# A gated attention layer: 36 of a group's 48 context products alternate one by one with the products of three W tiles

## The chip, the cores and the metric

The kernel runs on one core of one Trainium2 chip. Its engines are PE (TensorE, matmuls; its weight loads are shown as PEld), DVE (VectorE), ACT (ScalarE), POOL (GpSimd) and SP (SyncE, which here issues DMAs). They run side by side and order their work by semaphores: an instruction waits until a counter has reached a value, and another raises the counter when it is done. Each engine takes its own instructions in program order. The metric is the device time of one execution in microseconds (us), the median of several.

## What is computed

x and the context are 64 x 128 x 512 in float32. Cut to what matters here:

```python
def xattn(x, k, v, Wh, wg_w, wo_w, gamma, beta):     # k = v = context
    Q, K, V = (einsum('bshd,hde->bshe', t, Wh) for t in (xh, kh, vh))    # 4 heads of 128
    scores = einsum('bshe,bthe->bhst', Q, K) / sqrt(hd)
    A = maximum(abs((scores * D).sum(axis=0)), 1.0)   # summed over all 64 batches
    O = einsum('hst,bthe->bshe', A, V)
    Y = (O - mean) / sqrt(var + 1e-3) * gamma + beta
    return relu(x @ wg_w) * Y @ wo_w

x = x + tanh(g_xattn) * xattn(layernorm(x), ctx, ctx, ...)
x = x + tanh(g_ffn) * ffn(layernorm(x), gate, up, down, ...)    # 512 -> 1408 -> 512
```

The attention matrix A needs the sum over all 64 batches, so the kernel has a first part that goes through every batch, and only then can make O. The change is in the first part only.

## The kernel before

The 64 batches (tiles, t) are taken in 16 groups g of four. For each group the first part makes, from the normalized and transposed x (xnt) and the transposed context (ct):

- **z**, four sets of products, z(4g) to z(4g+3), one for each head: x times Wh Wh^T. Three float16 products of 512 columns each (high by high, high by low, low by high), written to the two PSUM banks pz[0] and pz[1] in turn (both lie in the tensor po). ACT copies the high part out (z_hi, L710), DVE makes the low part (z_lo, L1129), which also frees the bank: z(n) waits for z_lo(n-2).
- **v**, one per tile: for each of four heads three products in float32 (two parts of ct by 256 columns, of which 128 are Wh and 128 are z), into ps[t % 2]. v(t, 0) is heads 0 and 1, v(t, 1) heads 2 and 3: six products each, 48 a group. v(t, half) waits for the z_lo of its heads, for ct_lo (POOL), and for the bank: v_out(t-2) and v_acc(t-2). ACT's v_out (L735) copies V out of the bank to tmp, v_store (L747) sends it to the scratch in DRAM, and DVE's v_acc (L1159) adds the scores to a sum.
- **w**, one per tile: relu(x @ wg). Four blocks k of three float16 products of 512 columns into the bank pyb; ACT's w_out (L743) takes the relu to tmp, and w_store (L751) sends it off. w(t) waits for w_out(t-1).
- **rows(u)**, one per two tiles: four small transposes that spread mean and 1/std (POOL's rstd_pair) into ptb. DVE's normal(u) (L1125, four operations) then normalizes the transposed x, ACT's x_hi (L700) and POOL's x_lo (L1715) split it into xnt for the next group, and z of the next group waits for the last x_lo.
- ct_hi (ACT, L706) and ct_lo (POOL, L1721) split the context of the next group.

The order of every engine is written out by hand. On PE, group g (1 to 13) is: z(4g), z(4g+1), rows(2g+2), three blocks of w(4g-1), z(4g+2), z(4g+3), the last block of w(4g-1), v(4g, 0), v(4g+1, 0), v(4g, 1), v(4g+1, 1), rows(2g+3), w(4g), v(4g+2), w(4g+1), v(4g+3), w(4g+2). In group 1 rows(5) comes behind w(4). Group 14 has only two w tiles there, group 15 is shorter. LATE is 58; the w tiles from there on come behind the groups.

DVE's order in a group is: z_lo(4g), z_lo(4g+1), normal(2g+2), z_lo(4g+2), z_lo(4g+3), low_sums (some groups), stats(4g+8), v_acc(4g), v_acc(4g+1), normal(2g+3), stats, scale_tops (g = 10) or scale_powers (g = 13), low_weights(g-2, 0) (g = 2 to 13: L1213, and for the first eight chunks also L1222), wo_limit, wg_top (g = 8, 9), v_acc(4g+2), stats, low_sums (some), v_acc(4g+3), stats(4g+11) (g up to 13), low_weights(g-2, 1), wo_lo (L1245, g = 4 to 7) or wg_top (L1248, g = 8, 9). These side jobs look at the weights of the second part. stats are L1101 and L1103.

ACT's order is: four z_hi, w_out(4g-1), x_hi, w_store, x_hi, v_out(4g), v_out(4g+1), the two v_store, two ct_hi, w_out(4g), x_hi, w_store, x_hi, v_out(4g+2), w_out(4g+1), v_store, v_out(4g+3), w_store, v_store, wo_hi (g = 3 to 6), two ct_hi, w_out(4g+2), w_store.

SP loads the context and x for the coming groups, each load as soon as its buffer is free (for the context: when ct_lo is done), and for g = 9 to 13 parts of down_t that low_weights looks at.

## Time and profile before

| | us |
|---|---|
| three runs | 1441.26, 1441.88, 1445.92 |
| median | 1441.88 |
| span of the profiled execution | 1447.4 |
| PE busy in it | 1420.4 (98%) |
| PE weight loads (PEld) | 728.3 (50%) |
| DVE | 1043.3 (72%) |
| POOL | 735.3 (51%) |
| ACT | 726.3 (50%) |
| first part, groups 1 to 14 (34.07 to 311.66) | 277.6 |

The page's busy line for PE is at nine tenths or more in nearly every fortieth of the span, and the granted clock is near full throughout. Of the chain that ended last 74% is PE's. A busy share is a mean over stages, so the rows below are of the stage that the change touches. Matmuls overlap: one lasts 0.38 us in a row, but the next starts after 0.216 us, so starts are to be compared, not durations. A group of matmuls in the timeline runs until the start of the next, not for the duration shown. After a wait, or behind a product of another kind, the recorded start of a v product can be early.

### The profile page before, as it was taken

How to read it: one execution, taken by the hardware profiler on the slowest of the kernel's cores; microseconds unless marked ns; L12 is line 12 of the kernel's file. 1: busy time of each engine (PE TensorE's matmuls, PEld its weight loads, DVE VectorE, ACT ScalarE, POOL GpSimd, SP SyncE). 2: the span in 40 equal slices, each digit the busy share in tenths (PEclk: the TensorE clock that was granted, in tenths of full speed). 3: DMA queues.
4: the chain of work that ended last, by engine and by line, in shares of the span. 5: the costliest groups of instructions: out<-in, count | busy, mean ns of one | idle time of the engine just before them, and what ended most of it. 6: DMA issues, size and time to landing. Idle time of an engine off the chain costs nothing.

```text
span 1447.4 us, 20320 instructions
## 1 busy us (share of the span) xinstructions
PE 1420.4 (98%) x7097; PEld 728.3 (50%) x7135; DVE 1043.3 (72%) x1562; ACT 726.3 (50%) x1145; POOL 735.3 (51%) x734
## 2 busy tenths in 40 slices
PE   8999999999999999999999999999999999999998
PEld 4666666665445544455444444444444444444443
DVE  7788998878477676766776677564867768768762
ACT  5566565554555635455463545534344444443442
POOL 5656769863564445444553554434137237137235
PEclk9999999999999999999999999999999999999999
DMA  8999898973878796987888897886383473572432
GB/s 275 344 336 306 292 317 318 343 251 130 276 204 263 227 276 206 260 276 210 248 274 237 264 243 222 247 252 164 112 228 115 124 224 122 139 218 98 139 109 89
DMA packets 372920, 324.96 MB, mean 225 GB/s; under 512 B 259280, under 2 KB 285264, under 8 KB 372816
## 3 DMA queue, kind: packets, MB, share of 16 engines
q1 hardware_dynamic: 355248, 291.63, 66.2%
q10 hardware_dynamic: 17568, 31.99, 6.2%
q8 instruction: 59, 0.97, 0.3%
q14 instruction: 45, 0.37, 0.1%
HBM read 209.14 MB, written 114.43 MB: 224 GB/s over the span
## 4 chain that ended last, share of the span: by engine, by line
PE 74%; DVE 10%; DMA 6%; SPq 3%; issue 3%; ACT 2%; POOL 2%; ACTq 0%; DVEq 0%; POOLq 0%
PE ps L2067 24%; PE po L2067 8%; PE pyb L1930 7%; PE ps L2074 7%; PE ptb L2074 5%; PE pyb L2074 5%; PE ps L1988 5%; PE po L1930 3%; PE pyb L2058 3%; PE ptb L2058 3%; DMA wy_scratch<-misc 2%; SPq L510 2%; DVE reg L1129 1%; PE ptb L2062 1%; PE pyb L2062 1%
## 5 line engine op out<-in xcount | busy, mean ns | idle before, releaser
L2067 PE MATMUL ps<-x2t,gate 128*128 128x512 f16 x704 | 166.6, 379 | 1.2 <-DVE tmp L1436 1.1
L1930 PE MATMUL pyb<-xnt,wgs 128*128 128x512 f16 x708 | 166.3, 380 | 1.4 <-DVE wgs L1153 1.3
L2067 PE MATMUL ps<-op,wbuf 128*128 128x512 f16 x704 | 166.3, 379 | 0.5 <-issue 0.5
L2067 PE MATMUL ps<-x2t,up 128*128 128x512 f16 x704 | 166.3, 379 | 0.0
L1800 POOL TENSOR_TENSOR p5b<-p5b,p1b 128x512 f32<-128x512 f32 x44 | 55.7, 1265 | 209.1 <-ACT p5b L860 209.1
L1816 POOL TENSOR_TENSOR hid<-tmp,hid 128x512 f16<-128x512 f32 x88 | 104.6, 1190 | 105.9 <-ACT hid L836 105.9
L2074 PE MATMUL ps<-down_first,hid 128*128 128x512 bf16 x683 | 152.4, 379 | 2.1 <-POOL hid L1816 0.8
L1811 POOL TENSOR_TENSOR hsp<-hall,hsp 128x640 f16<-128x640 f32 (+2 forms) x72 | 123.6, 1731 | 37.1 <-ACT hsp L887 37.1
L2067 PE MATMUL po<-op,wbuf 128*128 128x512 f16 x528 | 129.0, 379 | 0.6 <-DVE u2b L1383 0.6
L1436 DVE SCALAR_TENSOR_TENSOR tmp<-ps,colsb,tmp 128x512 f32<-128x512 f32 x88 | 65.4, 744 | 68.2 <-PE ps L2067 62.3
L1988 PE MATMUL ps<-reg 128*128 128x256 f32 x768 | 109.7, 294 | 4.3 <-DVE reg L1129 3.8
L2067 PEld LDWEIGHTS ps<-op,wbuf 128*128 128x128 bf16 x704 | 68.5, 98 | 84.4 <-issue 2.5
L1760 POOL TENSOR_TENSOR wy_part<-raw,wy_part 128x1024 f16<-128x1024 f32 x30 | 66.0, 2201 | 87.6 <-ACT wy_part L825 87.6
L2067 PEld LDWEIGHTS ps<-x2t,up 128*128 128x128 bf16 x704 | 68.8, 98 | 82.9
L907 ACT ACTIVATE tmp<-ps,colsb 128x512 f32<-128x512 f32 x88 | 60.3, 685 | 99.2 <-PE ps L2067 99.1
L2074 PEld LDWEIGHTS ps<-down_first,hid 128*128 128x128 f16 x704 | 68.1, 98 | 83.4 <-POOL hid L1816 2.0
L2067 PEld LDWEIGHTS ps<-x2t,gate 128*128 128x128 bf16 x704 | 67.0, 98 | 81.0 <-DVE tmp L1436 1.8
L1988 PEld LDWEIGHTS ps<-reg 128*128 128x128 f32 x768 | 98.4, 190 | 13.3 <-DVE reg L1129 5.7
L1930 PEld LDWEIGHTS pyb<-xnt,wgs 128*128 128x128 f16 x708 | 66.4, 98 | 73.7 <-DVE wgs L1153 2.6
L1721 POOL TENSOR_TENSOR reg<-raw,reg 128x512 fp32r<-128x512 f32 x60 | 75.4, 1280 | 39.5 <-ACT reg L706 39.5
L1403 DVE TENSOR_TENSOR nbuf<-po,p1b 128x512 f32<-128x512 f32 x44 | 30.4, 692 | 78.5 <-PE po L2067 78.5
L887 ACT CAST hsp<-hall 128x640 f16<-128x640 f32 (+2 forms) x72 | 48.7, 712 | 71.2 <-PE pyb L2074 36.7
(218 smaller groups left out, 2764.2 us busy)
## 6 DMA issues: line engine op xcount, KB each, us to landing
wbuf<-ws_scratch SPq DMA_DIRECT2D x44, 896.0 KB, 5.0
xr<-in_x SPq DMA_DIRECT2D x62, 512.0 KB, 6.3
raw<-in_ctx_t SPq DMA_DIRECT2D x32, 512.0 KB, 5.6
v_scratch<-tmp ACTq DMA_DIRECT2D x64, 256.0 KB, 6.0
raw<-v_scratch SPq DMA_DIRECT2D x32, 512.0 KB, 6.6
x_scratch<-xr SPq DMA_DIRECT2D x32, 512.0 KB, 4.8
xr<-x_scratch SPq DMA_DIRECT2D x32, 512.0 KB, 5.9
raw<-w_scratch SPq DMA_DIRECT2D x31, 512.0 KB, 6.0
```

The source lines that it names most:

```text
L907: e.activation(tmp[:, m % 3, :], banks[2 * (n % 2)], ACT.Silu, scale=colsb[:, j:j + 1]).then_inc(s["si"])
L1436: e.scalar_tensor_tensor(tmp[:, m % 3, :], banks[2 * (n % 2) + 1], colsb[:, NI + j:NI + j + 1], tmp[:, m % 3, :], ALU.mult, ALU.mult).then ...
L1721: e.tensor_tensor(ct[g % 2][1][:, h, :], raw[:, h, :], f(ct[g % 2][0][:, h, :]), ALU.subtract).then_inc(s["ctlo"])
L1760: e.tensor_tensor(wyt[1][:, :, :], wt_of(q), wyt[0][:, :, :], ALU.subtract).then_inc(s["wylo"])
L1800: e.tensor_tensor(p5b[n % 2][:, :], p5b[n % 2][:, :], p1b[n % 2][:, :], ALU.add).then_inc(s["p15"])
L1811: e.tensor_tensor(hsp[t % 2][1][:, i0:i1, :], hall[:, i0:i1, 128 * i:128 * i + 128], hsp[t % 2][0][:, i0:i1, :], ALU.subtract).then_inc(s[ ...
L1816: e.tensor_tensor(hid[1][m % 11], tmp[:, m % 3, :], hid[0][m % 11], ALU.subtract).then_inc(s["hlo"])
L1930: last = e.matmul(dst, lhs[a], rhs[b], start=(k == 0 and i == 0), stop=(k == n - 1 and i == 2))
L1988: last = e.matmul(ps[t % 2][:, h, :, :], ct[g % 2][i][:, h, 128 * b:128 * b + 128], wh_and_z(q, h, b), start=(n == 0), stop=(n == 2))
L2058: e.matmul(py(t), wyt_of(t)[0][:, k, :], wos[i][k], start=(k == 0 and i == 0), stop=False)
L2067: last = e.matmul(dst, upper(wt), act[i], start=start, stop=stop and exact, skip_group_check=True)
L2074: last = e.matmul(dst, act, packed, start=start, stop=stop and exact)
```

## The change

It touches PE's order, ACT's order and the banks of W. In the full groups (g = 1 to 13) v(4g+1, 0), v(4g, 1), v(4g+1, 1), v(4g+2, 0), v(4g+2, 1) and v(4g+3, 0), 36 products, alternate one by one with the 36 products of w(4g), w(4g+1) and w(4g+2). v(4g, 0) stands alone ahead of them and v(4g+3, 1) behind them. rows(2g+3) comes in the middle. Group 14 has 18 such pairs. w(4g) and w(4g+1) (tiles 4 to 56) go to the banks pz[0] and pz[1] of z, so w(4g) waits for z_lo(4g+2), w(4g+1) for z_lo(4g+3), and z(4g+4), z(4g+5) wait for w_out(4g), w_out(4g+1). w(4g+2) and w(4g+3) stay in pyb. On ACT, w_out(4g) goes between v_out(4g) and v_out(4g+1), w_out(4g+1) ahead of v_out(4g+2), and two ct_hi, wo_hi and w_out(4g+2) ahead of v_out(4g+3). The order of DVE, POOL and SP is the same. The computation is the same.

```diff
         def pw(t):
+            if 4 <= t < LATE - 1 and t % 4 < 2:
+                return pz[t % 4]
             if t <= LATE:
                 return pyb[:, :]
@@ ACT, group g
-                v_out(4 * g)
-                v_out(4 * g + 1)
+                if more and g < NG - 2:
+                    v_out(4 * g)
+                    w_out(4 * g)
+                    v_out(4 * g + 1)
+                else:
+                    v_out(4 * g)
+                    v_out(4 * g + 1)
...
                 if g < NG - 2:
-                    w_out(4 * g)
+                    w_store(4 * g)
                 x_hi(2 * g + 3, 0)
-                if g < NG - 2:
-                    w_store(4 * g)
                 x_hi(2 * g + 3, 1)
+                w_out(4 * g + (1 if g < NG - 2 else 0))
                 v_out(4 * g + 2)
-                w_out(4 * g + (1 if g < NG - 2 else 0))
+                w_store(4 * g + (1 if g < NG - 2 else 0))
                 v_store(4 * g + 2)
-                v_out(4 * g + 3)
-                w_store(4 * g + (1 if g < NG - 2 else 0))
-                v_store(4 * g + 3)
+                ct_hi(g + 1, 2)
+                ct_hi(g + 1, 3)
                 if 3 <= g < 7:
                     wo_hi(g - 3)
-                ct_hi(g + 1, 2)
-                ct_hi(g + 1, 3)
                 if g < NG - 2:
                     w_out(4 * g + 2)
+                v_out(4 * g + 3)
+                if g < NG - 2:
                     w_store(4 * g + 2)
+                v_store(4 * g + 3)
@@ PE, z(n)
+                if h < 2 and 8 <= n < LATE + 3:
+                    p.wait_ge("wev", n - 3)
@@ PE, v(t, half, beside)
+                if beside:
+                    w_ready(*beside)
+                for n in range(6):
+                    h, (i, q) = 2 * half + n // 3, ((0, 0), (1, 0), (0, 1))[n % 3]
+                    last = e.matmul(ps[t % 2][:, h, :, :], ct[g % 2][i][:, h, 128 * b:128 * b + 128],
+                                    wh_and_z(q, h, b), start=(n % 3 == 0), stop=(n % 3 == 2))
+                    if half and n == 5:
+                        last.then_inc(s["v"])
+                    if beside:
+                        w_term(beside[0], beside[1][n // 3], n % 3)
+
+            def w_ready(t, ks):
                 x_ready(t // 4)
-                if 0 < t <= LATE:
+                if t in (1, 2, 3):
+                    p.wait_ge("wev", t)
+                elif 4 <= t < LATE - 1:
+                    p.wait_ge(*(("zlo", t + 3) if t % 4 < 2 else ("wev", t - 2) if t % 4 == 2 else ("wev", t)))
+                elif LATE - 1 <= t <= LATE:
                     p.wait_ge("wev", t)
@@ PE, group g
-                if g > 1:
-                    rows(2 * g + 3)
-                if g < NG - 2:
-                    w(4 * g)
-                if g == 1:
-                    rows(5)
-                v(4 * g + 2, 0)
-                v(4 * g + 2, 1)
-                w(4 * g + (1 if g < NG - 2 else 0))
-                v(4 * g + 3, 0)
+                full = g < NG - 2
+                v(4 * g, 0)
+                v(4 * g + 1, 0, (4 * g, (0, 1)) if full else None)
+                v(4 * g, 1, (4 * g, (2, 3)) if full else None)
+                v(4 * g + 1, 1, (4 * g + 1, (0, 1)) if full else (4 * g, (0, 1)))
+                rows(5 if g == 1 else 2 * g + 3)
+                v(4 * g + 2, 0, (4 * g + 1, (2, 3)) if full else (4 * g, (2, 3)))
+                v(4 * g + 2, 1, (4 * g + 2, (0, 1)) if full else None)
+                v(4 * g + 3, 0, (4 * g + 2, (2, 3)) if full else (LATE - 1, (0, 1)))
                 v(4 * g + 3, 1)
-                if g < NG - 2:
-                    w(4 * g + 2)
-                else:
-                    w(LATE - 1, (0, 1))
```

## Rows read from the trace of the kernel before

**Rows 1.** By group: us, busy (x) PE, PEld, DVE, ACT, POOL; PEclk, DMA share, GB/s.

```profile
134.31:154.81 20.50, 19.86 (x117) 12.61 (x116) 18.08 (x32) 12.79 (x24) 15.48 (x15) 1.00 0.88 296
...
294.07:311.66 17.59, 16.35 (x100) 10.81 (x99) 15.41 (x26) 9.93 (x17) 14.91 (x13) 1.00 0.61 202
sum 277.59, PE 273.06 PEld 175.70 DVE 240.97 ACT 166.57 POOL 203.37; mean PE 19.50 PEld 12.55 DVE 17.21 ACT 11.90 POOL 14.53
```

**Rows 2.** Timeline of DVE and of PE in a heavy group; start us, us, what, idle before.

```profile
135.50 1.84 DVE L1245 SCALAR_TENSOR_TENSOR wos<-up,wo_lim,wos 128x512 f16<-128x512 f32 x1
137.27 1.27 DVE L1129 TENSOR_TENSOR reg<-po,reg 128x512 fp32r<-128x512 f32 x2
...
142.18 1.70 PE L1988 MATMUL ps<-reg 128*128 128x256 f32 x12 [0.64 <-DVE reg L1129]
```

**Rows 3.** Timeline of PE around the start of group 10.

```profile
212.24 2.76 PE L1930 MATMUL pyb<-xnt,wgs 128*128 128x512 f16 x12
214.84 1.46 PE L1930 MATMUL po<-xnt,gs 128*128 128x512 f16 x6
...
218.51 1.46 PE L1930 MATMUL po<-xnt,gs 128*128 128x512 f16 x6
219.81 0.81 PE L1930 MATMUL pyb<-xnt,wgs 128*128 128x512 f16 x3
220.27 3.22 PE L1988 MATMUL ps<-reg 128*128 128x256 f32 x24
223.33 0.38 PE L1950 MATMUL ptb<-ident,mv 128*128 128x128 f32 x2
```

**Rows 4.** Timeline of DVE over the same stretch.

```profile
213.05 0.69 DVE L1159 TENSOR_TENSOR misc<-misc,ps 128x512 f32<-128x512 f32 x1 [0.24 <-ACT tmp L735]
...
214.48 0.85 DVE L1213 TENSOR_REDUCE lowbits<-up 128x1 f32<-128x704 uint16 x1
...
216.74 1.29 DVE L1129 TENSOR_TENSOR reg<-po,reg 128x512 fp32r<-128x512 f32 x2
217.95 2.47 DVE L1125 TENSOR_TENSOR xn<-xn,ptb 128x512 f32<-128x512 f32 x4
220.34 1.28 DVE L1129 TENSOR_TENSOR reg<-po,reg 128x512 fp32r<-128x512 f32 x2
```

**Rows 5.** Timeline of PE and of its weight loads (PEld), short windows at two edges.

```profile
206.56 0.38 PE L1930 MATMUL pyb<-xnt,wgs 128*128 128x512 f16 x1
...
206.89 0.19 PEld L1988 LDWEIGHTS ps<-reg 128*128 128x128 f32 x1
...
208.08 0.28 PE L1988 MATMUL ps<-reg 128*128 128x256 f32 x1
...
208.20 0.10 PEld L1930 LDWEIGHTS pyb<-xnt,wgs 128*128 128x128 f16 x1
...
208.43 0.10 PEld L1930 LDWEIGHTS pyb<-xnt,wgs 128*128 128x128 f16 x1
```

**Rows 6.** Timeline of ACT, the copy v_out(39).

```profile
212.43 0.58 ACT L735 COPY tmp<-ps 128x512 f32<-128x512 f32 x1 [0.74 <-PE ps L1988]
```

**Rows 7.** Stores of V from tmp, 102.9 to 292.3 us: issue to landing.

```profile
DMA to landing us min/median/max: 2.0/6.2/10.2
```

**Rows 8.** Timeline of DVE in groups 10 and 13, the two blocks of scales.

```profile
228.79 0.80 DVE L1168 SCALAR_TENSOR_TENSOR mags<-colsb 128x22 f32<-128x22 f32 x1
...
231.46 0.88 DVE L1213 TENSOR_REDUCE lowbits<-misc 128x1 f32<-128x704 uint16 x1
...
287.69 1.50 DVE L1188 TENSOR_REDUCE inv<-tops 128x6 f32<-128x768 f32 x1
...
292.19 0.87 DVE L1213 TENSOR_REDUCE lowbits<-misc 128x1 f32<-128x704 uint16 x1
```

**Rows 9.** A long gap of PE, and granted clock (PEclk) in the stage behind it.

```profile
772.14 2.15 PE L2058 MATMUL pyb<-wos,wy_part 128*128 128x512 f16 x6 [2.77 <-ACT wy_part L825]
...
772.00:776.00 4.00, 3.86 (x11) 1.52 (x12) 3.93 (x6) 1.03 (x2) 3.75 (x3) 0.60 0.85 142
```

More of the change, by code:

```diff
@@ L1923, in _, with three @@
             p = Program(e, s)
-            def three(dst, lhs, rhs, k, n, low=None):
+            def three(dst, lhs, rhs, k, n):
                 for i, (a, b) in enumerate(((0, 0), (0, 1), (1, 0))):
-                    if i == 2 and low:
-                        p.wait_ge(*low)
                     last = e.matmul(dst, lhs[a], rhs[b], start=(k == 0 and i == 0), stop=(k == n - 1 and i == 2))
@@ L1974, in first_z, with v @@
                             last.then_inc(s["z"])
-            def v(t, half):
+            def v(t, half, beside=None):
                 g, b = divmod(t, 4)
@@ L1985, in v @@
                     p.wait_ge("acc", t - 1)
-                for h in (2 * half, 2 * half + 1):
-                    for n, (i, q) in enumerate(((0, 0), (1, 0), (0, 1))):
-                        last = e.matmul(ps[t % 2][:, h, :, :], ct[g % 2][i][:, h, 128 * b:128 * b + 128],
-                                        wh_and_z(q, h, b), start=(n == 0), stop=(n == 2))
-                if half:
-                    last.then_inc(s["v"])
-            def w(t, ks=range(4)):
-                x_ready(t // 4)
-                if 0 < t <= LATE:
+                if beside:
[9 more added lines that the diff above has]
+            def w_ready(t, ks):
+                x_ready(t // 4)
+                if t in (1, 2, 3):
[3 more added lines that the diff above has]
+                elif LATE - 1 <= t <= LATE:
                     p.wait_ge("wev", t)
@@ L2003, in w, with w_term @@
                     p.wait_ge("vev", B)
-                for k in ks:
-                    if t == 0:
-                        p.wait_ge("scaledhi", k + 2)
-                    last = three(pw(t), [q[:, k, 128 * (t % 4):128 * (t % 4) + 128] for q in wgs],
-                                 [q[:, k, :] for q in xnt[t // 4 % 2]], k, 4, ("scaledlo", k + 2) if t == 0 else None)
-                if 3 in ks:
-                    last.then_inc(s["w"])
+            def w_term(t, k, i):
+                a, b = ((0, 0), (0, 1), (1, 0))[i]
+                if t == 0:
+                    p.wait_ge("scaledhi", k + 2)
+                    if a:
+                        p.wait_ge("scaledlo", k + 2)
+                last = e.matmul(pw(t), wgs[a][:, k, 128 * (t % 4):128 * (t % 4) + 128], xnt[t // 4 % 2][b][:, k, :],
+                                start=(k == 0 and i == 0), stop=(k == 3 and i == 2))
+                if k == 3 and i == 2:
+                    last.then_inc(s["w"])
+            def w(t, ks=range(4)):
+                w_ready(t, ks)
+                for k in ks:
+                    for i in range(3):
+                        w_term(t, k, i)
             def o(q):
@@ L2280, in _ @@
                     w(4 * g - 1, (3,))
-                v(4 * g, 0)
-                v(4 * g + 1, 0)
-                v(4 * g, 1)
-                v(4 * g + 1, 1)
                 if not more:
+                    v(4 * g, 0)
+                    v(4 * g + 1, 0)
+                    v(4 * g, 1)
+                    v(4 * g + 1, 1)
                     w(LATE - 1, (3,))
@@ L2291, in _ @@
                     break
-                if g > 1:
-                    rows(2 * g + 3)
-                if g < NG - 2:
-                    w(4 * g)
-                if g == 1:
-                    rows(5)
-                v(4 * g + 2, 0)
-                v(4 * g + 2, 1)
-                w(4 * g + (1 if g < NG - 2 else 0))
-                v(4 * g + 3, 0)
+                full = g < NG - 2
+                v(4 * g, 0)
+                v(4 * g + 1, 0, (4 * g, (0, 1)) if full else None)
[5 more added lines that the diff above has]
+                v(4 * g + 3, 0, (4 * g + 2, (2, 3)) if full else (LATE - 1, (0, 1)))
                 v(4 * g + 3, 1)
-                if g < NG - 2:
-                    w(4 * g + 2)
-                else:
-                    w(LATE - 1, (0, 1))
             w(LATE)
```

## The prediction

> **What bounds the kernel now.** I read the stages first, then the order of work inside one group, then the waits at its edges. The view of the groups takes the stretches from one z(4g) to the next; group k stands for g = k. Groups 1 to 14 take 277.59 us, and PE is busy in 273.06 of it, while DVE is busy 240.97 [rows 1]. A light group takes 19.58 us with no gap on PE; a heavy one (134.31 to 154.81) takes 20.50 [rows 1], and the 0.92 more is one gap, in which v(4g, 1) waits for z_lo(4g+3) (ahead of 142.18) [rows 2]. So the first part is PE's, with DVE just behind it in groups 5 to 8. The rest of the kernel isn't touched, and I move it whole.
>
> Inside a group: z(4g), z(4g+1), rows(2g+2), nine products of w(4g-1), then z(4g+2) comes 3.67 us after z(4g) (214.84 to 218.51); z, z and three w products more take 1.95; then 24 v products from 220.46 (219.81 plus three w at 0.216) to 223.33, which is 0.1195 us each; a w product takes 0.216 (six z in 1.30) [rows 3]. The last twelve w products of the group start at 212.24, so the last v is done 2.6 us before the next group starts at 214.84 [rows 3]. DVE's order is fixed by its program: v_acc(4g+3), stats, low_weights(g-2, 1), wo_lo or wg_top, and only then z_lo of the next group. In the trace v_acc(39) starts at 213.05, that is 1.79 before the group, low_weights at 214.48, z_lo(40) at 216.74, normal at 217.95, z_lo(42) at 220.34 [rows 4].
>
> **The change, part by part. 1, the pair on PE.** Each full group (g = 1 to 13) turns 36 v products in runs into v, w, v, w. No row shows such a row of singles, but both of its edges are there. A weight load starts with the product ahead of its own, so a load's start marks that product's start. From a w to a v: the last w starts at 206.56, the second v at 206.89, and 0.334 is 0.216 + 0.118: the f32 weights of the first v are loaded behind the w. From a v to a w: the v starts at 208.08, the f16 load only at 208.20, and the second w at 208.43, so v and w together take 0.349 instead of 0.120 + 0.216 [rows 5]. I found the same 0.348 to 0.349 at every one of these edges, also where the load has no wait of its own. Weights in f16 are thus not loaded while an f32 v product streams, and a v ahead of a w costs 0.133, 0.013 more than a v ahead of a v. 36 pairs cost 36 x 0.013 = 0.47 more per group, 6.3 us in 13 full groups and the 18 pairs of group 14. The bounds: if the load hides, the v takes the 0.109 of 256 columns (half of 0.216 and a little), the pair 0.325 and the group 36 x 0.024 = 0.86 less than I say; above, nothing points past 0.349. I take 0.349, since its rows are the very pair.
> The Trainium skill (TensorE: Matmul & The Clock Gate, "What happens when you issue a matmul") says the next tile's weights load while the current matmul runs, through a read port of their own. By it the pair would be 0.325. The rows at 208.08 to 208.43 don't agree for f32 followed by f16.
>
> **2, where the last v goes.** This is the large term, and it isn't on PE. Before, w(4g+2) came after v(4g+3, 1). Now it is woven in before it, and v(4g+3) ends where the next group begins. v_out starts 0.32 after the last v product starts (that is 0.13 ahead of the w at 212.24, so 212.11, and v_out 212.43 [rows 6]), and v_acc 0.62 after v_out (213.05). The last v product starts 0.13 before the new group, so v_acc(4g+3) can start 0.81 after the group's start, where it stood 1.79 before it: 2.6 us later. Nothing in DVE's program was moved, so all that is queued behind v_acc comes later by as much. Let A be the start of z_lo(4g), counted from z(4g). A = 0.81 + 1.43 for v_acc and stats (213.05 to 214.48) = 2.24; plus low_weights 1.56 (of 214.48 to 216.74, the rest is wg_top) where it has both reductions (groups 3 to 10) or 0.80 with one (11 to 14); plus wo_lo 1.77 (137.27 less 135.50, groups 5 to 8) or wg_top 0.70 (9 and 10) [rows 2, 4].
> z(4g+2) needs z_lo(4g) and can start 0.74 after it starts. In groups 5 to 8 that was met to the tick (137.27 + 0.74 = 138.01, the group's start plus 3.69). Now PE waits there: A + 0.74 against 3.68.
>
> **3, the new wait of w(4g).** It writes the bank of z(4g+2), so v(4g+1, 0) with its first w waits for z_lo(4g+2), which DVE starts 3.60 after z_lo(4g) because normal(2g+2) lies between (216.74 to 220.34 [rows 4]). PE may go on at A + 3.60 + 0.74 = A + 4.34. Queued behind that wait are all later products of the group. PE itself would be there at A + 0.74 + 1.95 + 0.72 = A + 3.41, so this costs 0.93 more in a group already late. What follows is 18 pairs (6.27), rows (0.44), 18 pairs, six v (0.73): 13.7. The period of a full group is therefore A + 18.05. The old wait of v(4g, 1) for z_lo(4g+3), worth 0.9 in groups 5 to 7, 0.5 in 8 and 0.9 in 11, is covered: v(4g, 1) now comes 2.1 us later.
>
> **4, ACT, POOL, SP.** Let V be the start of v(4g, 0). Six v and 18 pairs later, less the last pair, v(4g+1) is done; v_out takes it at V + 7.0, v_acc at 7.6, normal(2g+3) starts at V + 8.2 (rows(2g+3) is done by 7.7) and ends at 10.6; x_hi ends about V + 11.2, x_lo about V + 13.5 (two at 1.15), and z needs it at V + 14.5. This is nothing, by 1 us. ACT then has v_out(4g+2) at 11.8, two ct_hi, w_out(4g+2) at 13.9, v_out(4g+3) at 14.65: on time, except that wo_hi (0.6, groups 4 to 7) now stands ahead of the last two and delays them 0.45. v_store(4g) has 4.1 us until v_out(4g+2) wants its buffer; such stores landed in 2.0 to 10.2, median 6.2 [rows 7], and the long ones fall beside SP's loads, which now come only at V + 10.7 or later, behind ct_lo(g+1, 1). I take nothing, and up to 1.2 us a group for the upper bound.
>
> **5, DVE late in the middle.** normal(2g+3) ends at V + 10.6; stats, low_weights, wg_top, v_acc, stats and low_sums follow. In g = 8 and 9 they end 0.57 after v_acc(4g+3) could start. In g = 10 the scales (228.79 to 231.46, 2.67) make it 1.75, and the load of down_t that low_weights waits for another 0.75. In g = 13 scale_powers (287.69 to 292.19, 4.50) makes it 3.7 [rows 8].
>
> **The sum.** Periods A + 18.05: group 2 (A 2.24) 20.3; 3 (3.8) 21.9; 4 (4.25) 22.3; 5 to 7 (6.0) 24.1 each; 8 (5.6) 23.6; 9 and 10 (5.05) 23.1 each; 11 (5.5) 23.6; 12 and 13 (3.5, with 0.45 for the load) 21.5 each. Group 1 21.3 (only the new wait, about half a us). Group 14 keeps 12 v products together, A is 7.1 and the rest 13.8: 20.9 against 17.59 [rows 1]. Together 315.4, less 277.59, is 37.8; group 15 gives back 0.5, since it waited for late z_hi. Of the 37.8 some 6 are the pairs on PE, the others waits.
> The clock: PE will stand 2.6 to 3.6 us at z(4g+2) in groups 5 to 8 and 14. Once the trace shows such a gap, 2.77 us before 772.14, and behind it the granted clock is 0.60 in 772 to 776, the lower level 1.2 GHz for most of it [rows 9]: about 1.7 us lost. Here at most five such gaps, and the wait for z_lo(4g+2) takes up 0.9 of each loss; I add 1 us of a possible 8. The Trainium skill (TensorE: Matmul & The Clock Gate, "Why this matters for your kernels") warns of gaps of this length, and the row agrees.
> The execution profiled has a span of 1447.4 and the runs a median of 1441.88, 5.5 less; the differences are of one execution's groups and carry over. 1441.9 + 38 = 1480.
>
> **Rivals.** (a) The pair is 0.325 and the waits are as above: 36 x 0.024 x 13, and 0.4 in group 14, give 11.6 back: 1468. For it: the w-to-v edge hides its load. Against: every v-to-w edge [rows 5]. (b) PE alone counts: the waits on DVE don't appear, because v_acc isn't as late as I put it. Then 6 us for the pairs, less some 5 for the old waits: within 1442 to 1450. Against: six v products are all that PE does after the last woven pair. (c) Dearer: stores land late for v_out and w_out (1.2 us in ten groups) or the clock falls at all five gaps: 1492 to 1500. (d) The other side: the f16 load hides behind v. Before, the v's were bound by their loads (0.120 against 0.109), so 486 pairs save 0.011 each, 5.3 us, and the old z_lo(4g+3) waits of 5 go too: 1431. It decides only if z_lo(4g) starts within 2.94 us of the group, and with low_weights A is 3.8 in all of groups 3 to 10. (e) The change does what it says; PE's order can't be otherwise.
>
> **How the numbers follow.** Forecast 0.62, (a) 0.15, (b) 0.07, (c) 0.12, (d) 0.04. The range goes from 1460, (a) with a few us less of waits, to 1494, the lower part of (c); outside lie (b), (d) and half of (c). About 0.3% (4 us) is what a measurement here can tell from no change. Faster 0.04 is (d); same 0.03 is part of (b); slower 0.93.
>
> **What would show it.** On PE single v and w in turn, 0.349 from v to v (0.325 by (a)). A gap ahead of z(4g+2), released by z_lo, of 2.3 to 3.1 us in groups 5 to 8 and near 0 in group 2; a second of 0.9 at v(4g+1, 0). v_acc(4g+3) 0.8 after z of the next group. Periods of 21 to 24 us. The prediction is wrong if the periods stay near 20: then DVE had the z_lo's done earlier than its program order lets me think, or v_out didn't come last.

## The result, and the profile after

The changed kernel takes 1483.21 us (median; 1480.43 to 1484.19) against 1442.49 for the kernel before on the same chip (1441.26 to 1445.92): a ratio of 1.0277, 95% interval 1.0259 to 1.0296. It is slower by 40.7 us; 1480 was forecast, in a range of 1460 to 1494.

The head of the page of the kernel after: busy time of each engine, share of the span, instructions; then the chain that ended last by engine; then the line of v.

```profile
PE 1429.8 (96%) x7097; PEld 722.5 (49%) x7135; DVE 1038.7 (70%) x1562; ACT 725.4 (49%) x1145; POOL 734.5 (50%) x734
...
PE 69%; DVE 13%; DMA 5%; ACT 4%; issue 3%; SPq 3%; POOL 2%; ACTq 0%; DVEq 0%
...
L1997 PE MATMUL ps<-reg 128*128 128x256 f32 x768 | 213.1, 403 | 12.1 <-DVE reg L1135 10.2
```

The stages of the kernel after, with columns as in [rows 1]: a heavy group (6), a light one (12), group 14, all of groups 1 to 14, and the rest.

```profile
144.86:167.95 23.09, 20.47 (x119) 12.22 (x117) 16.99 (x32) 12.59 (x24) 15.22 (x15) 1.00 0.71 259
...
284.35:305.56 21.21, 20.36 (x119) 12.22 (x118) 15.13 (x27) 11.56 (x21) 17.33 (x16) 1.00 0.83 301
326.77:349.58 22.81, 17.65 (x101) 11.10 (x100) 18.15 (x29) 10.62 (x19) 17.47 (x14) 0.93 0.52 173
34.94:349.58 314.64, 283.61 (x1607) 170.06 (x1608) 236.01 (x423) 165.86 (x294) 202.38 (x192) 0.99 0.77 278
349.58:1482.30 1132.72, 1116.49 (x5337) 535.74 (x5372) 775.58 (x1085) 540.01 (x814) 513.81 (x514) 1.00 0.69 202
```

Groups 1 to 14 took 277.59 us before [rows 1] and take 314.64: 37.05 more, of which PE is busy for 10.6 (283.61 less 273.06) and idle for the other 26.5. DVE has the same instructions in them and is busy for 5 us less (236.01 against 240.97; 3.8 of the 5 are the four wo_lo, which last shorter, see part 2 below), so the loss isn't work, it is order. Another 0.9 lies ahead of group 1, where the executions of all kernels here differ by as much. The rest of the kernel is 3.0 shorter than in the profiled execution of before, which was 5.5 us above its own median. In the fourteen profiled executions of this study the rest takes 1129.0 to 1135.7 us, and that of the kernel before is the longest, so I read nothing into the 3.0.

Which waits they are, by the view of waits of the whole kernel after (line, waited for, us in total, times, longest):

```profile
PE po L1934 <- DVE reg L1135: 19.6, 13, 3.5
PE ps L1997 <- DVE reg L1135: 10.2, 12, 0.9
...
PE ps L1997 <- ACT tmp L745: 1.6, 1, 1.6
```

The first two, z and v waiting for z_lo, are 1.4 and 3.8 us in the kernel before. They stand at the two places that the prediction names: ahead of z(4g+2) in groups 1, 3 to 11 and 14, and at v(4g+1, 0) in all full groups but 2 (0.85 each). The third is a single wait for w_out(56) in group 14, which nobody forecast. The timeline of PE in group 6 (start, us, what, count, idle before):

```profile
146.59 2.11 PE L2027 MATMUL pyb<-xnt,wgs 128*128 128x512 f16 x9
150.47 1.47 PE L1934 MATMUL po<-xnt,gs 128*128 128x512 f16 x6 [1.77 <-DVE reg L1135]
...
154.15 0.36 PE L1997 MATMUL ps<-reg 128*128 128x256 f32 x1 [0.85 <-DVE reg L1135]
154.34 0.39 PE L2027 MATMUL po<-xnt,wgs 128*128 128x512 f16 x1
154.38 0.47 PE L1997 MATMUL ps<-reg 128*128 128x256 f32 x1
154.69 0.39 PE L2027 MATMUL po<-xnt,wgs 128*128 128x512 f16 x1
154.73 0.47 PE L1997 MATMUL ps<-reg 128*128 128x256 f32 x1
```

and of DVE in the same group, which began at 144.86:

```profile
146.08 0.69 DVE L1165 TENSOR_TENSOR misc<-misc,ps 128x512 f32<-128x512 f32 x1 [0.94 <-ACT tmp L737]
...
147.50 0.85 DVE L1219 TENSOR_REDUCE lowbits<-up 128x1 f32<-128x704 uint16 x1
148.27 0.88 DVE L1228 TENSOR_REDUCE wmax<-up 128x1 f32<-128x704 f32 x1
149.07 0.74 DVE L1251 SCALAR_TENSOR_TENSOR wos<-up,wo_lim,wos 128x512 f16<-128x512 f32 x1
149.72 1.28 DVE L1135 TENSOR_TENSOR reg<-po,reg 128x512 fp32r<-128x512 f32 x2
...
153.31 1.28 DVE L1135 TENSOR_TENSOR reg<-po,reg 128x512 fp32r<-128x512 f32 x2
```

v_acc(23) starts 1.22 behind the group's start (in the kernel before 1.79 ahead of it [rows 4]), z_lo(24) at 149.72, 4.86 behind it. z(26) starts at 150.47, 0.75 later, and v(25, 0) at 154.15, 0.84 after z_lo(26). The matmul ends are modelled, so I also take what a wait costs from the starts: nine w products from 146.59 would be over at 148.53, so the first costs 1.94; v(25, 0) comes 1.08 later than six v products of 0.120 behind the one before allow.

### The profile page after: what moved, and what is told of

Read it like the earlier page. It is cut to its first block, busy times and chain, and to the rows that moved or that the text cites. A ratio compares the mean times of both kernels' runs of the same rounds, so it can differ in the third digit from the quotient of the medians.

```text
span 1482.3 us, 20333 instructions
## 1 busy us (share of the span) xinstructions
PE 1429.8 (96%) x7097; PEld 722.5 (49%) x7135; DVE 1038.7 (70%) x1562; ACT 725.4 (49%) x1145; POOL 734.5 (50%) x734
## 4 chain that ended last, share of the span: by engine, by line
PE 69%; DVE 13%; DMA 5%; ACT 4%; issue 3%; SPq 3%; POOL 2%; ACTq 0%; DVEq 0%
PE ps L2093 24%; PE po L2093 8%; PE ps L2100 6%; PE ptb L2100 5%; PE pyb L2100 5%; PE po L2027 4%; PE ps L1997 4%; PE pyb L2084 3%; PE ptb L2084 3%; PE po L1934 2%; DMA wy_scratch<-misc 2%; DVE xr L1131 2%; SPq L512 2%; DVE reg L1135 2%; PE pyb L2027 1%
## 5 line engine op out<-in xcount | busy, mean ns | idle before, releaser
L1997 PE MATMUL ps<-reg 128*128 128x256 f32 x768 | 213.1, 403 | 12.1 <-DVE reg L1135 10.2
L1997 PEld LDWEIGHTS ps<-reg 128*128 128x128 f32 x768 | 135.4, 196 | 18.2 <-issue 14.7
L2027 PE MATMUL po<-xnt,wgs 128*128 128x512 f16 x324 | 114.2, 390 | 0.0
L2027 PE MATMUL pyb<-xnt,wgs 128*128 128x512 f16 x384 | 111.6, 384 | 1.2 <-DVE wgs L1159 1.1
L1165 DVE TENSOR_TENSOR misc<-misc,ps 128x512 f32<-128x512 f32 x63 | 43.2, 686 | 76.7 <-ACT tmp L737 76.5
```

Source lines behind the costliest of these rows:

```text
L1997: last = e.matmul(ps[t % 2][:, h, :, :], ct[g % 2][i][:, h, 128 * b:128 * b + 128], wh_and_z(q, h, b), start=(n % 3 == 0), stop=(n % 3 == 2))
L2027: last = e.matmul(pw(t), wgs[a][:, k, 128 * (t % 4):128 * (t % 4) + 128], xnt[t // 4 % 2][b][:, k, :], start=(k == 0 and i == 0), stop=(k ...
```

## The experiments

All ratios are against the kernel before on the same chip (1442 to 1443 us). The runs are spread over several chips, so two experiments are compared by their ratios, or by their traces. "z(60)" is the start of group 15 in the profiled execution: 311.66 in the kernel before, 349.58 in the one after. It measures the part that was changed alone. A is the start of z_lo(4g) counted from the group's start, as in the prediction. Two questions are asked: is it the pairs on PE or the waits on DVE, and is one cause of a wait worth its whole length?

**e1_blocks: 36 edges made 6.** In v(), the w products of a half first, then the v products.

```diff
+                for n in range(6) if beside else ():
+                    w_term(beside[0], beside[1][n // 3], n % 3)
                 for n in range(6):
...
-                    if beside:
-                        w_term(beside[0], beside[1][n // 3], n % 3)
```

> The changed kernel, but each of the six mixed stretches of a group has its six W products first and then its six v products, instead of one by one. All waits, banks and the order of the stretches stay. Edges from a v to a W product fall from 36 to 6 in a group. Theory (the waits on DVE's queue make most of the loss, the pair 0.349 instead of 0.336 the rest): 30 x 0.013 = 0.39 us less in each of 13 full groups, 0.2 in group 14, about 1478 us; the gap ahead of z(4g+2) stays (1.95 us in groups 6 and 7). Rival (alternating one by one is itself what costs, on PE or in the banks): most of the 41 us come back, 1445 to 1455.

Measured: 1482.34 us, ratio 1.0272 (1.0250 to 1.0293), z(60) at 350.24. The 5 us of the theory didn't come, and the rival that saw the pairs as the cause is far off. Group 6, by stage:

```profile
142.54:165.52 22.98, 19.93 (x119) 12.82 (x118) 17.00 (x32) 12.59 (x24) 15.19 (x15) 1.00 0.74 261
```

PE is busy for 0.54 less than in the kernel after (20.47), and the group is only 0.11 shorter (22.98 against 23.09): A has gone from 4.87 to 5.30. From v(4g, 0) to v_acc(4g+3) it is 16.6 us here and 16.7 there (group 6). That stretch, v, v_out, v_acc, normal, x_hi and v again, sets when z_lo can come, and the six v products at the end of each block end as late as those of the pairs do (reckoned: 18 x 0.349 less the last w's 0.216 is 6.07; 18 x 0.336 plus three edges of 0.013 is 6.09). The granted clock also fell behind three gaps (groups 7, 11 and 14), where it fell behind one in the kernel after (group 14), and groups 7 and 11 are 0.5 and 1.4 us longer. The other ten of groups 2 to 13 are together 1.3 shorter, where the theory has 3.9.

**e2_dve: DVE's queue mended.** v_acc(4g-1) behind z_lo(4g), z_lo(4g+1); its stats, low_weights, wo_lo and wg_top behind z_lo(4g+3).

```diff
                 z_lo(4 * g + 1)
+                if g > 1:
+                    v_acc(4 * g - 1)
...
                 z_lo(4 * g + 3)
+                if g > 1:
+                    if n + 3 < B:
+                        stats(n + 3)
+                    if 3 <= g < 15:
+                        low_weights(g - 3, 1)
+                    if 5 <= g < 9:
+                        wo_lo(g - 5)
+                    if g in (9, 10):
+                        wg_top(2 * g - 17)
...
-                v_acc(4 * g + 3)
-                if n + 7 < B:
-                    stats(n + 7)
-                if 2 <= g < 14:
-                    low_weights(g - 2, 1)
-                if 4 <= g < 8:
-                    wo_lo(g - 4)
-                if g in (8, 9):
-                    wg_top(2 * g - 15)
```

> The changed kernel with one difference, on DVE: v_acc(4g-1) stands behind z_lo(4g), z_lo(4g+1) of the next group instead of ahead of them, and stats, low_weights, wo_lo and wg_top of the group before stand behind z_lo(4g+3). PE, ACT and the banks as in the changed kernel. Theory (DVE's queue ahead of z_lo is what PE waits for): z_lo(4g) starts about 1.8 us after the group's start, no gap ahead of z(4g+2) except in groups 11 and 14, a gap of 0.6 at v(4g+1, 0) because v_acc now lies ahead of normal; periods near 20.7, in all some 25 us less, 1458 us (1454 to 1462). Rival (the late z_lo are a symptom, PE or ACT is late by itself): 1478 or more.

Measured: 1469.57, ratio 1.0176 (1.0159 to 1.0193), z(60) at 335.66. The gap at z(4g+2) is gone in groups 2 to 8, A is 1.8 to 2.3 there, and 13.6 us came back: the queue is a cause. But it isn't the 25 us that the sum of the gaps promised, and the reason is in the stages. Group 6, then group 9:

```profile
139.33:160.44 21.11, 20.28 (x119) 12.33 (x117) 18.09 (x32) 12.57 (x24) 15.29 (x15) 1.00 0.80 285
...
202.27:225.94 23.67, 20.63 (x119) 12.16 (x118) 19.78 (x34) 13.36 (x24) 14.29 (x15) 1.00 0.71 252
```

DVE is busy for 18 to 20 us in these groups, and what is moved back in its queue holds up something else. In group 6 v_acc(23) now stands ahead of normal, z_lo(26) starts at 145.81, and v(25, 0) waits 0.83 for it: all of the idle time in that group. Group 9 is a wait of another kind; the timeline of ACT:

```profile
201.77 0.59 ACT L737 COPY tmp<-ps 128x512 f32<-128x512 f32 x1 [2.17 <-DMA v_scratch<-tmp]
...
204.91 0.69 ACT L745 ACTIVATE tmp<-pyb,lim 128x512 f32<-128x512 f32 x1 [1.02 <-DMA w_scratch<-tmp]
```

v_out and w_out wait there for stores to land and free their buffer: the mechanism of rival (c), 3.2 us on ACT; groups 11 to 13 have one such wait each, of 0.8 to 1.5. Once the DVE wait is gone, this is what is next. It kept group 9 dear in the two kernels below that have the same order too (25.03 and 22.95).

**e3_banks: the gate of w(4g).** w(4g) back in pyb, w(4g+1) and w(4g+2) in the two banks of z.

```diff
-            if 4 <= t < LATE - 1 and t % 4 < 2:
-                return pz[t % 4]
+            if 4 <= t < LATE - 1 and t % 4 in (1, 2):
+                return pz[t % 4 - 1]
...
-                if h < 2 and 8 <= n < LATE + 3:
-                    p.wait_ge("wev", n - 3)
+                if h < 2 and 8 <= n < LATE:
+                    p.wait_ge("wev", n - 2)
...
-                    p.wait_ge(*(("zlo", t + 3) if t % 4 < 2 else ("wev", t - 2) if t % 4 == 2 else ("wev", t)))
+                    p.wait_ge(*(("zlo", t + 2) if t % 4 in (1, 2) else ("wev", t - 2) if t % 4 == 3 else ("wev", t)))
```

> The changed kernel with other banks: w(4g) in pyb, w(4g+1) in pz[0], w(4g+2) in pz[1], w(4g+3) in pyb, so w(4g) waits for w_out(4g-1) and no longer for z_lo(4g+2). Theory (that wait costs 1.08 us in every full group, as the trace of the changed kernel shows at v(4g+1, 0)): it goes, and w_out(4g-1), done about 1 us after v(4g, 0) starts, leaves 0.3; 0.75 less in 12 to 13 groups, about 1473 us. Rival (the wait only takes up time that the next one, v(4g, 1) for z_lo(4g+3) or v_acc, would take anyway): 1481 to 1484.

Measured: 1474.47, ratio 1.0211 (1.0180 to 1.0242), z(60) at 343.63: as the theory said. Groups 6 to 10, 12 and 13 are 0.69 to 0.71 shorter with A unchanged (group 6: 22.39, A 4.87). In groups 1 to 5, where A moved by up to 0.7, the gain is 0.96, -0.19, 0.44, 0.84 and 0.57; in group 11 the clock fell. It isn't the whole 1.08, since w(4g) now waits for w_out(4g-1) to empty pyb, 0.40 later than PE could start (row under e11_small_banks).

**e4_lastv: the last v back in its place.** w(4g+2) in one piece behind v(4g+3, 1), and v_out(4g+3) ahead of wo_hi, ct_hi and w_out on ACT. PE's part of the edit:

```diff
-                v(4 * g + 2, 1, (4 * g + 2, (0, 1)) if full else None)
-                v(4 * g + 3, 0, (4 * g + 2, (2, 3)) if full else (LATE - 1, (0, 1)))
+                v(4 * g + 2, 1)
+                v(4 * g + 3, 0)
                 v(4 * g + 3, 1)
+                if full:
+                    w(4 * g + 2)
+                else:
+                    w(LATE - 1, (0, 1))
```

> The changed kernel with only w(4g) and w(4g+1) woven in: v(4g+2, 1), v(4g+3, 0), v(4g+3, 1) stand alone and w(4g+2) behind them, as in the kernel before (group 14 likewise), and v_out(4g+3) stands ahead of ct_hi and w_out(4g+2) on ACT again. So v(4g+3) is done 2.6 us before the next group. Rival, the simple reading of my prediction (the place of the last v is all): z_lo(4g) comes 2.6 us earlier everywhere, 1450 us. Theory with both ends of DVE's queue: rows(2g+3) is still late, normal(2g+3), stats, low_weights, v_acc(4g+2), stats keep DVE busy until about 14.4 us after V, which is the group's end, so v_acc(4g+3) starts only 0.1 after the next group's start, 0.7 to 1.1 us earlier than in the changed kernel in groups 3 to 8, not in 9 to 11; with 12 edges fewer about 1474 us.

Measured: 1476.74, ratio 1.0228 (1.0207 to 1.0250), z(60) at 343.76. The theory's 1474 holds; the simple reading, that the last v's place is the whole loss, is wrong by 27 us. v_acc(4g+3) comes -0.4 to +0.4 from the group's start in groups 2 to 7 (0.55 to 1.22 before this edit), not the -1.79 of the kernel before, and in 8 to 10 no sooner at all: the gate of w(4g) has delayed every v of the group already, and what DVE owes from the middle of the group is still ahead of v_acc. The timeline of ACT and of DVE at the end of group 6 (group 7 starts at 163.53) shows it:

```profile
162.09 0.59 ACT L737 COPY tmp<-ps 128x512 f32<-128x512 f32 x1 [0.46 <-ACT tmp L737]
...
162.46 0.69 DVE L1164 TENSOR_TENSOR misc<-misc,ps 128x512 f32<-128x512 f32 x1
163.07 0.69 DVE L1106 BATCH_NORM_STATS2 st<-xr 128x6 f32<-128x512 f32 x1
...
163.89 0.67 DVE L1164 TENSOR_TENSOR misc<-misc,ps 128x512 f32<-128x512 f32 x1
```

v_out(27) is done at 162.68, but v_acc(27) starts at 163.89, behind v_acc(26) and its stats, with no idle time of DVE before it.

**e5_dve_banks and e7_dve_banks_blocks: mended together.** e5 is the edits of e2 and e3; e7 that and e1's.

> The changed kernel with both the DVE order of e2 and the banks of e3, the alternation one by one kept. Theory (the losses are waits in a loop through DVE): the gap ahead of z(4g+2) and the one at v(4g+1, 0) for z_lo(4g+2) are both gone or small, periods near 20.4 where DVE's middle isn't late (23 in group 9, 21 to 22 in 11, 13 and 14): about 1457 us. Rival (e2 and e3 take the same time away twice): 1468 or more.

Measured: 1467.51, ratio 1.0179 (1.0162 to 1.0195), z(60) at 335.57. Not 1457; the rival, one and the same slack, fits better, and the ratio can't be told from that of e2 (1.0176). Groups 2 to 8 are up to 0.6 shorter than in e2, 2.2 us in all, and group 9 (25.03 for 23.67) takes 1.4 of it back: z(37) waits 2.72 us there for w_out(34), which comes behind two waits of ACT for stores, and the granted clock is 0.57 in the 4 us behind that gap.

> As e5_dve_banks, with each mixed stretch as six W products and then six v products (as in e1). In e1 the 30 edges fewer gave no time back, since PE was waiting anyway. Theory (the pair's price of 0.013 us counts only where PE is the bound): here most periods are PE's, so 0.39 in some 8 to 10 groups, 3 to 4 us less than e5. Rival (the price isn't real, or is paid elsewhere): no difference, or more.

Measured: 1466.40, ratio 1.0167 (1.0152 to 1.0183), z(60) at 331.67, 3.9 sooner than in e5. In the trace the edges come through where PE is nearer to being the bound (group 3: 19.90 against 20.46), but 2.1 of the 3.9 lie in group 9, where the clock didn't fall this time. The medians of the two kernels are 1.1 apart with intervals that overlap, so I call this seen in one trace each, not measured.

**e6_before_dve: e2's order of the late jobs in the kernel before.** stats, low_weights, wo_lo and wg_top of the end of a group behind z_lo(4g+3) of the next, v_acc where it was (the lower half of e2's diff, without its v_acc lines).

> The kernel before with one change, on DVE: stats(4g-1), low_weights(g-3, 1), wo_lo and wg_top of the group before stand behind z_lo(4g+3) instead of ahead of z_lo(4g). PE, ACT, banks as before. Theory (even before, v(4g, 1) waits 0.9 us in groups 5 to 7, 0.5 in 8 and 0.9 in 11 for z_lo(4g+3), because these jobs stand ahead of it): these gaps go, periods 19.6, 4 to 5 us less than before, 1438 us. Rival (DVE is full in groups 5 to 9 in any order, 18.1 to 19.7 us busy in periods of 19.6 to 20.5): the gaps move to another place, within 1.5 us of before.

Measured: 1456.78, ratio 1.0102 (1.0084 to 1.0121): 14 us slower, and both sides missed it. The stage of group 8, and what PE waited for in it:

```profile
177.62:198.94 21.32, 20.04 (x118) 12.65 (x117) 19.30 (x32) 11.76 (x20) 14.77 (x15) 1.00 0.93 343
...
190.79 1.67 PE L1989 MATMUL ps<-reg 128*128 128x256 f32 x12 [1.17 <-DVE misc L1159]
```

The wait for z_lo(4g+3) went, as expected, and v(4g+2) now waits 1.17 for v_acc(4g). In its new place wo_lo runs beside POOL and lasts 1.68 (186.70), where alone it lasts 0.74 (see e8 and e9 below); that is 0.94 of the 1.17. So even in the kernel before DVE's queue has no place where 2 us of work can be put for nothing. A price read off as "work moved to where DVE is idle" was wrong twice, here and in e2.

**e8_small and e9_before_small: the side jobs cut, after and before.** In low_weights and low_sums, `704 * half + 704`, `stg[:, :]` and `n * quarter + n` become 64 columns; most of the look at W's low bits and maxima is left out. DVE's queue keeps its order and loses some 1.3 us of work ahead of z_lo(4g) where both reductions stand there.

> The changed kernel with DVE's side jobs low_weights and low_sums cut to 64 columns each (from 704, 640 or 768), so they leave out most of the look at the weights' low bits and maxima; nothing else differs. Theory (DVE's queue): low_weights falls from 1.56 to about 0.3, z_lo(4g) comes 1.3 us earlier in groups 3 to 10, the gap ahead of z(4g+2) goes in groups 3, 4 and 12, 13 and shrinks to 0.4 in 5 to 8; the 1.08 at v(4g+1, 0) stays in part: about 1460 us. Rival (PE order and banks by themselves): above 1478.

Measured: 1466.13, ratio 1.0176 (1.0145 to 1.0208), z(60) at 335.12: 17 us back, 6 fewer than the theory's 1460, and far from the rival. In groups 6 and 7 A falls only from 4.87 to 4.64, because wo_lo moves beside POOL (next rows).

> The kernel before with the look at W's low bits and maxima cut to 64 columns of each piece, as e8_small did to the kernel after: most of that look is left out. It says what the side jobs of VectorE cost the order before. Theory: in the kernel before they cost only the waits of 0.9 us in groups 5 to 8 and 11, so 1438 us, and the 23 us by which e8_small stands above the kernel before are the price of the new order itself. Rival: they cost the old order nothing either, 1442 to 1443. If it came to 1425 or less, the side jobs would bind the old order as well and the comparison with e8_small would have to be read anew.

Measured: 1439.58, ratio 0.9979 (0.9966 to 0.9991), z(60) at 308.46, as the theory said (1438). All full groups from 2 on now take 19.58 to 19.65. The same jobs cost the new order 17 us and the old one 3. That is the finding of the study in one pair: the jobs lay hidden behind PE, and the change uncovered them. It isn't the whole loss: the ratio of e8_small is still 1.0176.

This pair also shows what made wo_lo cost 1.8 us at one time and 0.7 at another. Timeline of DVE and POOL in e8_small:

```profile
143.05 1.84 DVE L1251 SCALAR_TENSOR_TENSOR wos<-up,wo_lim,wos 128x512 f16<-128x512 f32 x1
...
141.84 2.50 POOL L1727 TENSOR_TENSOR reg<-raw,reg 128x512 fp32r<-128x512 f32 x2
```

and in e9_before_small:

```profile
134.90 0.74 DVE L1245 SCALAR_TENSOR_TENSOR wos<-up,wo_lim,wos 128x512 f16<-128x512 f32 x1
...
135.04 2.96 POOL L1721 TENSOR_TENSOR reg<-raw,reg 128x512 fp32r<-128x512 f32 x2 [1.56 <-ACT reg L706]
```

Started while the first of ct_lo's two pieces runs on POOL, wo_lo lasts 1.84 and ends 0.55 behind the second; started 0.14 ahead of ct_lo it lasts 0.74, and the two pieces last 2.96 where they last 2.50 in e8_small. The Trainium skill (SBUF — State Buffer, "Who interferes with whom") says that a VectorE instruction with two inputs in SBUF and a GpSimd one that reads SBUF can't run side by side: whichever is issued second waits for the first. The rows of e9 agree: the first piece of ct_lo, begun behind wo_lo, lasts 1.74 for the second's 1.26. In e8 wo_lo waits for the piece that was running, as the page says, but also through the second piece, whose record starts 0.02 behind its own; that sentence doesn't explain the second wait.

**e10_before_zlo: a candidate.** The kernel before, in groups 5 to 8, 11 and 14 both z_lo's ahead of normal(2g+2).

```diff
-                if more:
+                first = g in (5, 6, 7, 8, 11, 14)
+                if more and not first:
                     normal(2 * g + 2)
                 z_lo(4 * g + 2)
                 z_lo(4 * g + 3)
+                if more and first:
+                    normal(2 * g + 2)
```

> The kernel before, in whose groups 5 to 8, 11 and 14 VectorE makes z_lo(4g+2) and z_lo(4g+3) ahead of the normalization of rows 2g+2, not behind it. Theory: v(4g,1) no longer waits 0.9 us there for z_lo, six groups at 0.9, and the normalization comes late enough to be needed by nobody sooner: 1438 us. Rival: VectorE has no slack there; what it does later for the rows makes the transposes or v_lo wait, and the time stays within 1.5 us of the kernel before or is slower, as with e6_before_dve.

Measured: 1444.37, ratio 1.0024 (1.0011 to 1.0038): the rival, by 2.1 us. The wait at v(4g, 1) went and another came, in group 6:

```profile
143.48 0.40 PE L1953 MATMUL ptb<-ident,mv 128*128 128x128 f32 x2 [0.37 <-DVE xr L1125]
```

the transposes for rows 2g+3, which want the normalization of rows 2g+2 done. DVE also stood idle 0.94 for z_hi ahead of z_lo(4g+2). Groups 1 to 14 take 277.5 us, as before (277.6). No kernel here beats the one before with all its work in place.

**e11_small_banks and e12_small_banks_blocks: what is left when DVE is out of the way.** e8's cut with e3's banks, and e12 with e1's blocks as well.

> The kernel after with the banks of e3_banks and the side jobs of VectorE cut as in e8_small (most of the look at W's low bits and maxima is left out). What is left against e9_before_small is the interleaving itself and the order of VectorE. Theory: the wait of w(4g) for z_lo is gone (0.7 us a group as in e3_banks): e8_small's 1466 less 7 to 8 is 1459 us. Rival: without the side jobs the gate was not the last thing to come, within 2 us of e8_small.

Measured: 1462.30, ratio 1.0136 (1.0115 to 1.0157), z(60) at 328.97, 6.2 sooner than e8_small; by the medians 3.8 less, half of the 7 to 8 expected, with intervals that overlap (1.0115 to 1.0157 against 1.0145 to 1.0208).

> As e11_small_banks, but each mixed stretch runs its six W products first and then its six context products, so 6 edges from context to W a group and not 36. Theory: with the side jobs and the bank wait gone TensorE is nearer to being the bound, and 30 edges at 0.013 us are 0.39 us in each of some 8 groups: 3 us less than e11_small_banks, 1456 us. Rival: the round of v_out, v_acc, normalization and v_out still sets the period, and the two kernels differ by less than 1 us, as e1_blocks and the kernel after did.

Measured: 1460.71, ratio 1.0131 (1.0114 to 1.0148), z(60) at 327.33. Over the whole kernel 1.6 us against 3, less than these intervals can tell. Light groups are clear, though. Group 12 of e9, of e11 and of e12:

```profile
252.53:272.11 19.58, 19.58 (x117) 12.72 (x116) 13.46 (x27) 11.66 (x20) 17.17 (x16) 1.00 0.96 325
...
265.99:286.44 20.45, 20.29 (x119) 12.33 (x118) 13.37 (x27) 11.53 (x21) 17.39 (x16) 1.00 0.84 310
...
263.34:283.24 19.90, 19.74 (x119) 12.86 (x118) 13.33 (x27) 11.34 (x21) 17.31 (x16) 1.00 0.86 322
```

Here PE has one short wait and no other, in e11 at

```profile
272.64 0.35 PE L1997 MATMUL ps<-reg 128*128 128x256 f32 x1 [0.16 <-ACT tmp L745]
```

which by the starts costs 0.40 (0.32 in e12). 19.58 + 0.40 + 36 x 0.013 is 20.45, what the group takes; with 6 edges 19.58 + 0.32 + 0.08 is 19.98 against 19.90. So an edge costs about what the prediction said, where PE is the bound. Beside that, e11 stands 20.5 us behind e9 at z(60): 12 groups at 0.87 are 10.4, group 14 is 5.4 (22.07 against 16.70), and the rest (less 0.9 in group 1) lies mostly in groups 5 to 7 and 11, where A still reaches 3.6 to 4.65.

## Why the prediction held, point by point

**The place of the loss** held. It was to be waits on z_lo and not PE's own time, and of the 37.05 us in groups 1 to 14 PE's busy time is 10.6.

**Part 1, the pair** held in size: from 154.38 to 154.73, 0.35, and sixteen pairs from 154.38 to 159.96 are 0.349 each. The weight loads in the same stretch tell why:

```profile
154.34 0.10 PEld L2027 LDWEIGHTS po<-xnt,wgs 128*128 128x128 f16 x1
154.34 0.20 PEld L1997 LDWEIGHTS ps<-reg 128*128 128x128 f32 x1
154.69 0.10 PEld L2027 LDWEIGHTS po<-xnt,wgs 128*128 128x128 f16 x1
```

The f32 load starts with the w product ahead of it (154.34), the f16 load only when that w product is due itself (154.69), not with the v product at 154.38. What failed is how the term was used. The 6.3 us were added to the waits as if they were apart from them. e1_blocks took 30 of the 36 edges away and gained 0.9 us (within the error), e11 against e12 shows the full price only in light groups. Rival (a), a pair of 0.325, is ruled out by the measured 0.349, and what it would have given isn't shown: with it the v products of each stretch would also have ended sooner (18 x 0.325 less 0.216 is 5.63, for 6.07), which e1's blocks don't do.

**Part 2, the queue** held, but for one term and one sign. For group 6, forecast and measured:

```
                                          forecast  measured
v_acc(4g+3) behind the group's start        0.81      0.81 (light groups)
wo_hi ahead of v_out(4g+3) on ACT           0.45      0.41 (1.22 in groups 4, 6, 7)
v_acc and stats                             1.43      1.42
low_weights, two reductions                 1.56      1.57
wo_lo                                       1.77      0.65   <- mis-sized
A                                           6.02      4.87
A to the next group's start (P - A)        18.05     18.22
period P                                   24.1      23.09
```

The mis-sized term is wo_lo. The row at 135.50 with its 1.84 us was taken for its duration. It was a duration with POOL in the way: ct_lo ran from 134.29 for 2.50 us in the kernel before, and in the kernel after, 3.0 us later against the group's start, wo_lo starts when ct_lo (146.52, two of 1.28) is through, and takes 0.74 in all four groups. This makes four groups 0.9 to 1.2 too dear in the forecast, 4.1 us together, and with it the sign that was to show it, a gap of 2.3 to 3.1 us ahead of z(4g+2) in groups 5 to 8, failed: the gaps are 1.35 to 1.78. One row of a two-input DVE instruction should have been compared with POOL's rows over the same stretch. The part also gave one reason for the late v_acc, the place of the last v. e4_lastv shows a second that reaches nearly as far: with the last v back, DVE's own jobs from the middle of the group still hold v_acc(4g+3) until -0.4 to +0.4 of the next group's start, where it stood at -1.79.

**Part 3, the gate** held: 1.08 in each full group from 3 on, for 0.93. e3_banks took 0.68 of it away (0.40 was left) and got 0.69 to 0.71 in seven groups: with A unchanged this wait is on the path by itself, unlike the pairs.

**Part 4** held in these groups: a store made v_out wait once in the kernel after (0.27 us at 324.50, in group 13), and x_hi and x_lo came in time. Waits of rival (c)'s kind, 1.2 us a group, were seen once e2 let PE run faster: 2.17 and 1.02 in one group, 0.8 to 1.5 in three more.

**Part 5**, DVE late in the middle, was too cheap in group 11: 24.48 for 23.6, with A at 6.27 for 5.5 (v_acc starts 2.68 behind the group's start). Group 14 took 22.81 for 20.9, but not by its A, which is 6.62 where the forecast puts 7.1 (its own terms, 2.24 + 0.80 + 3.7, give 6.74). What follows z_lo took 16.2 for 13.8. Timeline of PE, and in the last line the granted clock, in group 14:

```profile
334.13 2.74 PE L1934 MATMUL po<-xnt,gs 128*128 128x512 f16 x6 [3.52 <-DVE reg L1135]
...
346.68 0.35 PE L1997 MATMUL ps<-reg 128*128 128x256 f32 x1 [1.64 <-ACT tmp L745]
...
334.10:337.50 3.40, 3.37 (x10) 1.43 (x11) 3.40 (x6) 1.18 (x2) 3.32 (x2) 0.60 0.45 180
```

Six z products take 2.74 where they take 1.47 in group 6; about 1.4 us are the clock's, for a forecast 1 in the whole kernel. The other wait, 1.64 (about 1.9 by the starts), is v(59, 0), whose w products of tile 57 need w_out(56); ACT does that behind x_hi (345.86), which waits for DVE's normal. It is in no term of the prediction.

**The sum.** By group, forecast and measured: 1: 21.3, 22.01. 2: 20.3, 20.67. 3: 21.9, 21.76. 4: 22.3, 22.57. 5 to 7: 24.1 each, 22.91, 23.09, 23.09. 8: 23.6, 22.67. 9 and 10: 23.1 each, 23.15, 23.01. 11: 23.6, 24.48. 12 and 13: 21.5 each, 21.21 both. 14: 20.9, 22.81. Forecast 315.4 and measured 314.64 agree better than their parts: 4.1 us too much in groups 5 to 8 stand against 1.9 too little in 14, 0.9 in 11 and 0.7 in 1. That the total came within 1 us is partly luck. The medians differ by 40.7, which is 3.7 more than the groups account for. In these two traces 0.9 of it lies ahead of group 1; the other 2.8 is less than the scatter of what follows group 14 (1129.0 to 1135.7 us), so it says nothing about the change.

**How the 38 us at z(60) divide**, each step an edit that was run: 14.5 go when the side jobs are cut (e8; the same cut gives the old order 3.2), 6.2 more with the gate's bank (e11), 1.6 more with blocks for pairs (e12, seen in one trace each). 18.9 are left against e9; less the 3.2 these make 37.9. By the traces of e12 and e9, 7.4 of the 18.9 lie in group 14 (24.12 against 16.70) and 13.3 in groups 2 to 13, of which some 4.8 are the wait for w_out and the six edges and the others mostly waits for z_lo; group 1 gives 1.7 back. No run took these away, so for this half of the loss the cause is read from the waits and not shown by an edit.

## What to carry to other kernels

A job that costs nothing is hidden behind something. Before an edit that moves the last producer of a stage later, list the jobs that stand behind it in each in-order queue, and price them at their full length: the same side jobs cost 3 us in one order and 17 in the other. Waits at one round don't add up: take one away and the run tells how much of it the next one keeps (25 expected from the queue, 13.6 got; 14 us lost by a like move in the old kernel), and a saving on the engine that waits (0.5 us of pairs) may give nothing. And a duration read for a VectorE instruction with two inputs in SBUF isn't its own price while POOL's rows run beside it: wo_lo lasted 0.74 to 1.96 us in these traces.

## What the runs showed of the hardware

The weights of an f16 product weren't loaded while an f32 product of 256 columns streamed: the edge v to w costs 0.133 for 0.120 of v to v, at every one of the edges looked at, while f32 weights load behind an f16 product.

The granted clock didn't fall by the length of a gap alone. It fell (to a mean of 0.50 to 0.66 over the 4 us behind the gap) after idle times of 2.20 (group 7 of e1_blocks), 2.72 (group 9 of e5_dve_banks), 2.77 [rows 9], 3.00 (group 11 of e3_banks) and 3.52 (group 14 of the kernel after). It stayed at 1.00 behind 2.65 (group 14 of e11_small_banks), 2.88 (group 9 of e7_dve_banks_blocks) and 3.17 (group 11 of the kernel after). Three of them, from the kernel after, e3_banks and e1_blocks, each with the view of the 4 us behind the gap (granted clock in the third column from the end):

```profile
266.87 1.47 PE L1934 MATMUL po<-xnt,gs 128*128 128x512 f16 x6 [3.17 <-DVE reg L1135]
266.87:270.87 4.00, 3.14 (x18) 1.93 (x18) 4.00 (x7) 2.88 (x5) 3.11 (x3) 1.00 1.03 385
...
260.25 2.74 PE L1934 MATMUL po<-xnt,gs 128*128 128x512 f16 x6 [3.00 <-DVE reg L1135]
260.25:264.25 4.00, 4.00 (x10) 1.70 (x11) 4.00 (x7) 1.17 (x2) 2.71 (x2) 0.50 1.04 398
...
171.55 2.74 PE L1934 MATMUL po<-xnt,gs 128*128 128x512 f16 x6 [2.20 <-DVE reg L1135]
171.55:175.55 4.00, 4.00 (x13) 1.79 (x14) 4.00 (x7) 1.41 (x3) 1.70 (x1) 0.59 1.03 368
```

The same six products last 1.47 behind the longest of these gaps and 2.74 behind the shortest. What makes the difference I can't say from these runs; a few us of the scatter between the kernels come from it.
